# A ViT tower on one core: Mamba's inputs batch by batch, z of the second batch made inside the scan, and the projection and the last norm reordered

## The reference

```python
# h: (8, 513, 256), the residual stream behind layer 0 (attention, diagonal scan, quantised ffn)
x = _layernorm(h)
xz = x @ W_in.T
x_val, z = jnp.split(xz, 2, axis=-1)              # 512 channels each
xv = conv1d(x_val, taps=4, causal) + conv_b
x_val = _silu(xv)
A = -jnp.exp(A_log)                               # 512 x 16
dt = jax.nn.softplus(x[:, :, :64] @ W_dt.T + b_dt)
Bm = x @ W_B.T; Cm = x @ W_C.T                    # 16 columns each
# over tokens t: state n of 16, channel d of 512
h_t = exp(dt * A) * h_(t-1) + (dt * x_val) * Bm;  y_t = sum over n of h_t * Cm
h = h + (y * _silu(z)) @ W_out.T
h = h + _L1_ffn_ref(_layernorm(h), ...)           # quantised, gated ffn
```

## Time and profile before

| | |
|---|---|
| median of 3 executions | 2870.0 us (2860.18 to 2885.66) |
| the profiled execution | 2874.32 us, span of its instructions 2872.5 us |
| TensorE clock, mean over the span | 0.840 of full |
| busy share PE / DVE / ACT / POOL | 70% / 74% / 45% / 43% |
| one turn | about 705 us, of them about 197 us of scan |

### The profile page before, as it was taken

One profiled execution on the slowest core, in us unless ns is written; L12 is line 12 of the kernel. 1 busy time (PEld: TensorE's weight loads), 2 busy tenths in 40 slices (PEclk: granted clock), 3 DMA queues, 4 the chain that ended last, 5 costly groups with the idle time before them and its releaser, 6 DMA issues.

```text
span 2872.5 us, 22420 instructions
## 1 busy us (share of the span) xinstructions
PE 2015.8 (70%) x7684; PEld 1072.3 (37%) x7684; DVE 2128.5 (74%) x2457; ACT 1306.5 (45%) x1838; POOL 1243.8 (43%) x535
## 2 busy tenths in 40 slices
PE   3786486677597847677668774777767966667775
PEld 1125362226322625223532253422452234542243
DVE  7753868995684495998768367799686827689967
ACT  1363445553155335654306443665421645356532
POOL 1030238991213024997211311599521221079942
PEclk9798588998789868899879976799977987689997
DMA  5500000000330000000061000000006100000000
GB/s 172 90 18 0 1 1 0 0 1 0 80 77 7 0 0 0 0 0 1 0 118 45 1 1 0 1 0 0 0 1 118 46 1 1 0 0 0 0 0 15
DMA packets 55914, 57.45 MB, mean 20 GB/s; under 512 B 8624, under 2 KB 50352, under 8 KB 55792
## 3 DMA queue, kind: packets, MB, share of 16 engines
q1 hardware_dynamic: 48880, 49.62, 6.8%
q10 hardware_dynamic: 6912, 6.29, 1.9%
HBM read 38.71 MB, written 16.79 MB: 19 GB/s over the span
## 4 chain that ended last, share of the span: by engine, by line
PE 44%; DVE 25%; POOL 14%; issue 7%; ACT 5%; DMA 3%; SPq 1%; ACTq 0%; POOLq 0%; DVEq 0%
PE psum L571 15%; PE psum L776 10%; POOL big L1507 9%; PE psum L671 4%; POOL big L1496 4%; DVE mid L1110 3%; PE psum L648 3%; PE psum L659 3%; PE psum L609 3%; DVE mid L1324 2%; PE psum L681 2%; ACT mid L833 2%; DVE big L1275 2%; DMA mid<-scratch 2%; DVE big L1149 2%
## 5 line engine op out<-in xcount | busy, mean ns | idle before, releaser
L776 PE MATMUL psum<-big,ident 128*128 128x512 f32 x992 | 524.0, 677 | 202.7 <-POOL big L1507 202.1
L1390 DVE TENSOR_TENSOR_SCAN big<-psum,b,big 128x512 f32<-128x512 f32 x512 | 613.9, 1259 | 0.0
L833 ACT ACTIVATE big<-psum 128x1024 f32<-128x1024 f32 (+2 forms) x592 | 451.9, 776 | 324.2 <-PE psum L659 252.1
L1507 POOL TENSOR_TENSOR big<-big 128x2048 f32<-128x2048 f32 x124 | 560.7, 4522 | 22.3 <-DVE big L1390 22.3
L833 ACT ACTIVATE psum<-mid,aneg 128x512 f32<-128x512 f32 x512 | 353.9, 692 | 265.0 <-DVE big L1390 265.0
L776 PEld LDWEIGHTS psum<-big,ident 128*128 128x128 f32 x992 | 202.1, 214 | 483.1 <-POOL big L1507 264.6
L1201 DVE TENSOR_REDUCE negmax<-psum 128x1 f32<-128x512 f32 x512 | 317.0, 678 | 68.1 <-PE psum L648 67.8
L648 PE MATMUL psum<-mid 96*128 96x512 bf16 x512 | 221.5, 438 | 65.6 <-DMA mid<-scratch 51.0
L1458 POOL TENSOR_TENSOR lsum<-lsum,onorm 128x512 f32<-128x512 f32 x32 | 40.6, 1270 | 523.7 <-ACT onorm L833 523.7
L1496 POOL TENSOR_TENSOR big<-mid,big 128x512 f32<-128x512 f32 (+1 forms) x128 | 222.9, 1742 | 20.0 <-ACT big L833 20.0
L1472 POOL TENSOR_TENSOR big<-big,mid 128x513 f32<-128x513 f32 x40 | 55.0, 1387 | 348.4 <-ACT big L833 348.4
(11 more groups left out here) (165 smaller groups left out, 3393.1 us busy)
## 6 DMA issues: line engine op xcount, KB each, us to landing
mid<-scratch SPq DMA_DIRECT2D x192, 64.0 KB, 2.2
scratch<-mid SPq DMA_DIRECT2D x4, 1536.0 KB, 6.0
mid<-scratch SPq DMA_DIRECT2D x48, 128.0 KB, 11.7
mid<-scratch ACTq DMA_DIRECT2D x48, 128.0 KB, 13.7
scratch<-big SPq DMA_DIRECT2D x4, 1536.0 KB, 25.8
out<-hres SPq DMA_DIRECT2D x8, 513.0 KB, 7.7
big<-in_x SPq DMA_DIRECT2D x8, 512.0 KB, 4.1
big<-in_w SPq DMA_DIRECT2D x2, 1024.0 KB, 6.3
```

What stands on the lines that cost most here:

```text
L776: mm = nc.tensor.matmul(y_psum[:, c], ident[:, :], st(1, k)[:, c], start=(n == 0), stop=(n == NS - 1))
L833: return nc.scalar.activation(o, a, func, **kw)
L1390: V.tensor_tensor_scan(st(0, k)[:, c], a_psum(DT * k + c), st(0, k)[:, c], b0[:, p, n, c:c + 1], ALU.mult, ALU.add).then_inc(scanned, 1)
L1507: G.tensor_tensor(st(1, k), st(0, k), c_row(k).unsqueeze(1).broadcast_to([P, DT, S]), ALU.mult).then_inc(hc_ready, 1)
```

## The change

- `plan_fills` and PE's list: the order is d and x of batch 0, `bc` of both, d and x of batch 1, the product of the first token (now a fill, `first`, in a slot, no longer in the bank of the C rows), z of batch 0. ACT and DVE take them in that order; the softplus of a batch, its Exp and its Ln, now follow its own d products.
- `z0` to `z3` of batch 1 are made inside the scan, in slots 0 and 1 (the banks of the sum over states, which is not begun then): two behind `spread_c(0)`, two in step 0. ACT copies them unchanged (`take_z`) between the second and the third decay of step 0, and makes their SiLU behind its last decay, with two table loads around it.
- The start states of batch 1 are made by DVE at the beginning of step 14 (`first_states(1)`), the first outputs of a batch just before its gate (`first_output`). POOL's product dt times x of batch 1 (`inject(1)`) comes behind its first two `spread_pool`.
- Behind the scan PE projects batch 0 (`project(0, 0)`, `project(0, 1)`) before `add_y(30)` and the last sums; DVE adds it to the residual before its gates.
- The last norm is made batch by batch: mean of batch 0 before the projection of batch 1; then on DVE centre 0, residual 1, normalise 0, maximum 0, centre 1, scales 0, normalise 1, maximum 1, scales 1. PE's transposes follow both variances.

```diff
     ln(3)
-    each(*[f"d{c}" for c in range(DT)])
-    each("bc")
-    each(*[f"x{c}" for c in range(DT)])
-    each(*[f"z{c}" for c in range(DT)])
+    tiles("d", 0)
+    tiles("x", 0)
+    order.extend((("bc", 0), ("bc", 1)))
+    tiles("d", 1)
+    tiles("x", 1)
+    order.append(("first", 0))
+    tiles("z", 0)
+
+    for c in range(DT):
+        while len(order) % 4 != c % 2:
+            order.append(None)
+        order.append((f"z{c}", 1))
...
 # PE
+                def late_z(c):
+                    fill(f"z{c}", 1, [(wz[:, k, c * P:(c + 1) * P], big_un(1)[:, k]) for k in range(KT)])
...
                 spread_b(0)
                 spread_c(0)
+                late_z(0)
+                late_z(1)
                 spread_b(1)
                 for k in range(PAIR * NS):
                     if k + 2 < PAIR * NS:
                         spread_b(k + 2)
                     if k + 1 < PAIR * NS:
                         spread_c(k + 1)
-                    if k:
+                    if k == 0:
+                        late_z(2)
+                        late_z(3)
+                        pe.wait_ge(z_raw, DT)
+                    if 0 < k < PAIR * NS - 1:
                         add_y(k - 1)
...
+                pe.wait_ge(gated, 2 * (PAIR - 1))
+                pe.wait_ge(scanned, DT * NS * PAIR)
                 project(0, 0)
+                pe.wait_ge(c_copied, NS * PAIR)
+                pe.wait_ge(b_copied, NS * PAIR)
+                pe.wait_ge(tail_dve, DT - TAIL_DVE)
+                project(0, 1)
+                add_y(PAIR * NS - 2)
                 for n, c in enumerate(TAIL_ORDER):
...
-                project(0, 1)
-                pe.wait_ge(gated, PAIR - 1 + DT)
+                mean(4, 0, hres[:, 0])
+                pe.wait_ge(gated, 2 * (PAIR - 1) + 1 + DT)
                 project(1, 0)
                 project(1, 1)
-                layer_norm(4, lambda p: hres[:, p])
+                variance(4, 0)
+                mean(4, 1, hres[:, 1])
+                variance(4, 1)
                 token_maxima(2)
 # ACT
+                dt_in(0)
+                first_tap(0, 0)
+                first_tap(0, 1)
+                log_term(0)
+                first_tap(0, 2)
+                first_tap(0, 3)
+                dt_in(1)
+                log_term(1)
+                for c in range(DT):
+                    first_tap(1, c)
                 nc.scalar.preload_act_table(ACT.Silu)
...
+                def take_z(c):
                     wait_full(act, f"z{c}", 1)
-                    run(mid4(1, 1)[:, c], slot(f"z{c}", 1), ACT.Silu).then_inc(z_silu, 1)
+                    run(mid4(1, 1)[:, c], slot(f"z{c}", 1), ACT.Copy).then_inc(z_raw, 1)
...
                                 if k + 1 < PAIR * NS:
                                     copy_b(k + 1)
+                                if k == 0:
+                                    for z in range(DT):
+                                        take_z(z)
 # DVE
+                taps(0, 0)
+                round_term(0)
+                for c in range(1, DT):
+                    taps(0, c)
+                split_bc(0)
+                split_bc(1)
...
+                round_term(1)
+                taps(1, 0)
+                step_size(0)
+                for c in range(1, DT):
+                    taps(1, c)
+                step_size(1)
...
                 def gate(p):
 
+                    first_output(p)
                     dve.wait_ge(y_summed, NS * (p + 1))
...
+                def first_states(p):
+                    x0 = mid4(p, 3)[:, :, 0]
+                    dve.wait_ge(dtx_ready, p + 1)
+                    V.tensor_tensor(b0[:, p], x0.unsqueeze(1).broadcast_to([P, NS, DT]),
+                                    first[:, p, 0:NS].unsqueeze(2).broadcast_to([P, NS, DT]), ALU.mult).then_inc(
+                                        first_state, 1)
+
+                def first_output(p):
+                    x0 = mid4(p, 3)[:, :, 0]
+                    dve.wait_ge(z_silu, DT * (p + 1))
+                    V.scalar_tensor_tensor(out=mid4(p, 0)[:, :, 0], in0=x0, scalar=s0[:, p:p + 1],
+                                           in1=mid4(p, 1)[:, :, 0], op0=ALU.mult, op1=ALU.mult).then_inc(gated, 1)
...
                 for k in range(PAIR * NS):
                     p, n = divmod(k, NS)
+                    if k == NS - 2:
+                        first_states(1)
+                        dve.wait_ge(first_state, PAIR + 3)
...
 # POOL
-                pool.wait_ge(dtx_ready, PAIR)
+                inject(0)
+                pool.wait_ge(dtx_ready, 1)
                 spread_pool(0)
                 spread_pool(1)
+                inject(1)
+                pool.wait_ge(dtx_ready, 2)
                 for k in range(PAIR * NS - 1):
```

More of the change, by code:

```diff
@@ L108, in plan_fills, with tiles @@
     ln(3)
-    each(*[f"d{c}" for c in range(DT)])
-    each("bc")
-    each(*[f"x{c}" for c in range(DT)])
-    each(*[f"z{c}" for c in range(DT)])
+    def tiles(name, p):
+        order.extend((f"{name}{c}", p) for c in range(DT))
+    tiles("d", 0)
[9 more added lines that the diff above has]
+        order.append((f"z{c}", 1))
+    while len(order) % 4 != 2:
+        order.append(None)
     each("w0", "w1")
@@ L953, in _, with dt_in @@
                 layer_norm(3)
-                for p in range(PAIR):
+                def dt_in(p):
                     for c in range(DT):
@@ L984, in _ @@
-                    run(mid4(1, 0)[:, c], mid4(1, 0)[:, c], ACT.Silu).then_inc(m_silu, 1)
-                for c in range(DT):
-                    wait_full(act, f"z{c}", 1)
-                    run(mid4(1, 1)[:, c], slot(f"z{c}", 1), ACT.Silu).then_inc(z_silu, 1)
-                load_ln_exp()
-                act.wait_ge(first_full, 1)
-                run(first[:, :, :].rearrange("p b r -> p (b r)"), c_psum[:, 0:PAIR * 32], ACT.Copy).then_inc(
-                    first_copied, 1)
-                act.wait_ge(dt_ready, PAIR)
@@ L1356, in finish_scan @@
                         V.tensor_tensor(st(1, k)[:, c], st(0, k)[:, c], c_psum, ALU.mult).then_inc(tail_dve, 1)
+                    for c in range(KT):
+                        take_projected(0, c)
+                    first_output(PAIR - 1)
                     for n, c in enumerate(TAIL_ORDER):
```

229 lines of the change are left out of this document (128 added, 101 removed).

## The result

The changed kernel takes 2915.4 us (median of 4 runs, 2914.8 to 2916.4) against 2871.2 for the kernel before (4 runs, 2860.2 to 2885.7): a ratio of 1.015, 95% interval 1.013 to 1.018. That is slower by more than 1%, and above the range forecast, 2862 to 2910.

The account below looks back on a forecast made before the run. No engine bounds the whole; POOL sets the scan's pace. 0.6 + 3.0 + 1.4 = 5.0 us a turn, 20 in all, takes the profiled 2874.3 to 2894; the median lies 4.3 below, so 2890, range 2862 to 2910.

Parts of the forecast that it names:

- the term for the join: Where the scan's batches join: DVE's two tiny operations wait for POOL, +3.0 us a turn, bounds 0 and 4.5.
- the second part of the 3.0: Before the gate: `first_output(0)` waits for POOL's long product with C, to 1258.1; the gate starts there instead of at 1255.13.
- Inputs: From the first d product to POOL's first C product: early start given back, +0.6 us a turn.
- early gain: Start of the scan: first scan 2.2 to 3.9 us earlier, at 60.0 to 61.7 against 63.9.
- the third rival: Scan's start, chance 0.23: late z copies on a low clock, `spread_b(1)` waits 6.9 us, not 3.6, ACT's stall doubles; 2906.
- Behind the scan: From the last scan to the quantiser: serial work of two batches no longer pairs, +1.4 us a turn, bounds -1 and +4.
- the slow case: Quantiser's spread rows: 9.90 us against 5.98 by the clock; sparser PE makes it likelier, +0.3 in the mean.
- The silu, the table loads and the waits in `finish_scan`: Behind ACT's last decay and before the gates: covered by other waits, cost nothing; 5 us if ACT's cover went.
- The rival with 9 a turn: Slower by over 1%, chance 0.23: low clock at the late z, plus the join and slow rows, 2906.

Follow-up runs that it names:

- experiments 1 to 3: The changed kernel with batch 1's start states made by POOL, with batch 0's first outputs made before the scan, and with both: 2901.3, 2900.8 and 2890.6 us.
- experiment 7: The kernel before with one unused 32-element DVE product, both operands in SBUF, added at the head of step 14: 2888.2 us, ratio 1.006.
- experiment 12: The changed kernel with `first_output(0)` made before the scan and `first_states(1)` put behind the third scan of step 14: 2892.7 us, ratio 1.009.
- experiment 3: The changed kernel with batch 1's start states made by POOL and batch 0's first outputs made before the scan: 2890.6 us, ratio 1.007.
- experiment 4: The kernel of experiment 3 with ACT copying the late z of batch 1 in two portions, in steps 0 and 1: 2879.0 us, ratio 1.004.
- Experiment 5: The kernel of experiment 4 with the last norm of both batches made together again: 2857.5 us, ratio 0.994.
- experiment 1: The changed kernel with batch 1's start states made by POOL, behind `inject(1)`, instead of by DVE: 2901.3 us, ratio 1.011.

## Why the prediction was wrong

**The failed step is the price of `first_states(1)` in the term for the join.** The prediction saw the mechanism (a DVE instruction with both inputs in SBUF stands while POOL works), the places, and even the distance inside POOL's product (0.26 us, measured 0.26). It then let the operation in at the end of that product: 1.1 us, "nobody feels that yet, as it is less than its lead". It took 5.5 in every turn. The long case of L1364, and the L1275 stretch, where DVE got in ahead of POOL's next, were taken as a rule; there POOL had paused at most 8.6 us before. In the scan, where it hadn't for 73 us, the bound of 4.5 us for the whole join was one POOL instruction too low. Measured +7.5 a turn against +3.0 and its bounds 0 to 4.5. Why DVE is passed there stays open. `first_output(0)` took 3.8, and the second part of the 3.0 was right; experiments 1 to 3 put each operation's share on it, and experiment 7 the same 4.5 to 6.3 in a kernel that has nothing else of the change.

The Trainium skill, "SBUF — State Buffer", section "SBUF: two separate sides", says that whichever of the two starts first gets the pair for the whole instruction. The 455 samples that waited agree with that; in the 81 the two starts are too close to say which was first. The 32 don't follow from it, since DVE's operation was up before POOL's next one began and yet went behind it (experiment 12: up at 1244.77, POOL's next at 1245.62 first). The measurement decides.

**Inputs: +1.8 against +0.6, mechanism right.** Each step came within 1 us: taps at 11.4 (forecast 12.1), split at 21.4 (22.2), the cast that waits for POOL's sum 1.54 us, step sizes at 42.3 and 53.3 (42.3 and 53.7), first scan at 60.1 (60.0 to 61.7), ended early gain and all. The stall behind it is 3.8 in one turn, as forecast, and 5.5 in three, by the late z at 5.41 instead of 3.73. That was the third rival's mechanism, without its other half: `spread_b(1)` didn't wait for a low clock.

**Behind the scan: −0.3 against +1.4.** The serial norm costs what was said, rows 2.1 us later behind the projection (forecast 2.6). The projection ends 1.2 earlier in the mean (1.5). What wasn't there is the rest: the rows and products behind it took 1.3 less than before in the mean, not 0.3 more. The rows took 7.5, 7.2, 6.3 and 6.3 in the four turns, where before 9.9 and 6.0 alternated: the slow case that I made likelier never came in this execution. With the same order it did come in experiment 3 (10.0 in all four turns) and in two turns of experiment 4, so that the term came out at −0.3 is in part luck. Experiment 5 puts the pairing itself at some 5.4 a turn by the medians, more than the serial cost that I had counted (2.6).

**The silu, the table loads and the waits in `finish_scan`** cost nothing that shows, as said: the stretch to the last scan's end is 83.6 in both.

Sum: 7.5 + 1.8 − 0.3 = 9.0 a turn by the three terms, 8.8 by the whole table (the first half of the scan is 0.1 shorter), against 5.0. The rival with 9 a turn, 2906, had the right size for another reason. With the join at its true price my sum would have been 0.6 + 7.5 + 1.4 = 9.5 a turn and 2908, so the one term makes 18 of the 25 us between 2890 and 2915.4; some 5 of the rest lie outside the touched stages.

## What to carry to other kernels

A tiny operation isn't a cheap one if it needs a resource that a busy neighbour holds: in a stretch where POOL runs back to back, and DVE hasn't had such an instruction for long, price a DVE instruction with two SBUF inputs at what is left of POOL's current instruction and the next (3.1 to 6.4 us here, whatever its size), put it before the stretch, give it to POOL, or let one operand come from PSUM. Rows from one stretch don't price another where the neighbour runs without a pause. When a change of several parts loses, take it apart before dropping it: here two of its ideas, without the operations that rode along and without the unpaired norm, are 0.6% faster than the kernel before, part of which may be the clock of the rows.

## What the hardware showed that I had not expected

- A DVE product of 4 elements with both inputs in SBUF took 5.5 us beside POOL, with 32 elements 5.6 and with 64 5.5 to 6.4 (3.1 where only 0.9 was left of POOL's current instruction); with one input from PSUM 0.166.
- DVE's operation can be passed by a POOL instruction that starts 0.85 us after it came up (experiment 12), and by two (experiment 1, 5.93 us), all 32 times in stretches in which POOL had not paused for 73 us or more and DVE had run no instruction without a PSUM operand for 88.6, and in none of 536 where POOL had paused within the last 30.4 and DVE had run one within the last 21.3. Which of the two counts isn't known.
- The late z, the same 16 matmuls in the same place, took 3.73 us in one turn and 5.41 in three, which moved the whole scan by 1.7.
